# A hand-written order for two transformer layers: turns of TensorE in one piece, and other constants in the planner

## What is computed

```
for l in (0, 1):
    sa, ca, ga, sb, cb, gb = split(silu(c[l]) @ wmod[l])       # per batch, 256 each
    ga, gb = sign(ga) * max(|ga|, 0.25), sign(gb) * max(|gb|, 0.25)
    h = layernorm(x) * (1 + ca) + sa
    x = x + ga * attention[l](h)                               # 16 heads of 16, causal
    h = layernorm(x) * (1 + cb) + sb
    x = x + gb * ffn[l](h)
```

## Time and profile before

| | |
|---|---|
| median of 3 runs | 2705.45 us (2704.71 to 2705.87) |
| the profiled execution | 2702.86 us |
| its span, first to last instruction | 2701.1 us |
| mean granted clock of PE | 0.968 of full |
| PE busy | 2432.1 us (90%), 18968 matmuls |
| DVE busy | 2127.8 us (79%) |
| ACT busy | 1701.9 us (63%) |
| POOL busy | 1025.6 us (38%) |
| DMA | 218.38 MB, mean 81 GB/s |

### The profile page before, as it was taken

The page is one execution under the profiler, slowest core; times in us unless marked ns, Lnnn a source line. Parts: engine busy times, 40 slices in busy tenths (PEclk is TensorE's granted clock), DMA queues, the critical chain, the costliest instruction groups (busy, mean ns, idle before and its releaser), DMA issues. The chain is left out here.

```text
span 2701.1 us, 56435 instructions
## 1 busy us (share of the span) xinstructions
PE 2432.1 (90%) x18968; PEld 1023.9 (38%) x18968; DVE 2127.8 (79%) x6588; ACT 1701.9 (63%) x3458; POOL 1025.6 (38%) x1558
## 2 busy tenths in 40 slices
PE   7798888999999999999999999999999999898586
PEld 4323434324334343443434343343434434344223
DVE  3898738898887988879887888879888798862972
ACT  3476574576765667666676677666677666665164
POOL 4222452245332544236243453325342363326222
PEclk9999999999999999999999999999999999999798
DMA  6511134113322222322312133222223123002300
GB/s 219 166 58 35 38 109 119 47 44 103 105 81 75 79 88 89 92 72 83 116 61 83 51 102 105 83 81 72 91 88 102 60 83 109 21 31 74 97 2 16
DMA packets 142400, 218.38 MB, mean 81 GB/s; under 512 B 21190, under 2 KB 62556, under 8 KB 142052
## 3 DMA queue, kind: packets, MB, share of 16 engines
q1 hardware_dynamic: 142120, 214.77, 25.9%
HBM read 137.87 MB, written 77.89 MB: 80 GB/s over the span
## 5 line engine op out<-in xcount | busy, mean ns | idle before, releaser
L1208 ACT ACTIVATE probs<-big 128x512 f32<-128x512 f32 (+2 forms) x2560 | 1218.9, 573 | 457.1 <-PE big L1656 451.5
L1421 DVE CUSTOM_DVE_ANT_0 big<-big,mask 128x128 f32<-128x128 f32 (+3 forms) x2048 | 940.0, 518 | 157.3 <-PE big L1634 155.0
L1656 PE MATMUL big<-stack_q,stack_k 64*128 64x512 f16 (+3 forms) x6144 | 684.6, 330 | 69.6 <-DVE mx L1421 27.0
L1419 DVE TENSOR_REDUCE mx<-big 128x1 f32<-128x512 f32 x1024 | 644.0, 679 | 119.2 <-PE big L1634 115.1
L1675 PE MATMUL ctx_ps<-probs,v_ones 128*17 128x512 f32 (+3 forms) x6144 | 645.3, 501 | 28.2 <-POOL probs L1087 26.6
L1087 POOL TENSOR_SCALAR_AFFINE_SELECT probs<-probs 128x512 f32<-128x512 f32 x512 | 332.5, 660 | 591.1 <-ACT probs L1208 590.9
L1634 PE MATMUL big<-stack_k,stack_q 64*128 64x512 f16 (+3 forms) x3072 | 434.9, 332 | 74.7 <-DVE mx L1421 39.5
L1656 PEld LDWEIGHTS big<-stack_q,stack_k 64*128 64x128 f16 x6144 | 222.5, 94 | 668.9 <-issue 470.9
L1634 PEld LDWEIGHTS big<-stack_k,stack_q 64*128 64x128 f16 x3072 | 136.3, 94 | 410.8 <-issue 254.3
L1421 DVE DVE_READ_ACCUMULATOR2_ANT mx<- 128x1 f32 x2048 | 282.8, 138 | 0.0
L1580 PE MATMUL big<-hT,w_qkv 128*128 128x512 f32 x512 | 266.4, 629 | 1.4 <-DVE mx L1421 0.5
(11 more groups left out here) (94 smaller groups left out, 1923.3 us busy)
## 6 DMA issues: line engine op xcount, KB each, us to landing
image<-region SPq DMA_DIRECT2D x192, 256.0 KB
stack_q<-image SPq DMA_DIRECT2D x64, 512.0 KB, 3.7
stack_k<-image SPq DMA_DIRECT2D x64, 512.0 KB, 4.5
lo_dram<-region SPq DMA_DIRECT2D x64, 256.0 KB
w_qkv<-wqkv SPq DMA_DIRECT2D x16, 768.0 KB, 4.9
x_res<-x SPq DMA_DIRECT2D x32, 256.0 KB, 2.9
stack_q<-lo_dram SPq DMA_DIRECT2D x128, 64.0 KB, 3.8
stack_k<-lo_dram SPq DMA_DIRECT2D x128, 64.0 KB, 4.5
```

Of the source, the lines that this page charges most:

```text
L1208: s.activation(probs[:, n % HELD, heads, q0:], big[:, at.slot(turn), 0:len(pairs) * width] .rearrange("p (h q) -> p h q", h=len(pairs)), A ...
L1419: last = v.reduce_max(to, held, AX)
L1421: last = v.tensor_tensor_reduce(out=held, in0=held, in1=mask[:, BANK - width:], scale=1.0, scalar=3.0 * NEG, op0=ALU.add, op1=ALU.max, acc ...
L1656: last = te.matmul(big[:, at.slot(at.turn() + parity), j * width:(j + 1) * width], stack_k[rows, c, g * PAIR_N + pair, kt * P:(kt + 1) * P ...
```

## The change

The planner no longer puts halves into its queues: the `pre` and `post` queues hold each turn once, and `pe_time` gives it its whole cost. In the model, a link of the layernorm chain on POOL costs 200 ns of the engine and 85 ns on top until the next may begin, where it was 77 and 110 on both engines; on DVE it stays so. The constants `ROWS_FIRST`, `PHASES` and `FEED_WAIT` have other values. The instructions themselves are the same; only their order changes. (The added line moves all lines behind it by one: L1580 before is L1581 after.)

```diff
@@ pe_time
-    return pe_cost(item) / (2 if kind in HALVED else 1)
+    return pe_cost(item)
@@
-ROWS_FIRST = 445.6080
+ROWS_FIRST = 520.8978
@@
-PHASES = {"max": (-0.0897, 0.0000, 0.0000, 0.0000, 0.0000, 0.0000, 0.0000, 0.0514), ...
-FIRST_FEED, FEED_WAIT = {"max": 216.0, "score": 430.0}, 300.0000
+PHASES = {"max": (-0.0897, 0.0000, 0.0000, 0.1674, 0.0207, 0.0000, 0.0000, 0.0514), ...
+FIRST_FEED, FEED_WAIT = {"max": 216.0, "score": 430.0}, 264.0094
@@ Model.other, "ln"
-                self.ready["ln"] = self.ready["factors"] = self.run(engine, begin, 75 * (item[6] - item[5]) if n == 0 else 77, 110)
+                self.ready["ln"] = self.ready["factors"] = self.run(engine, begin, 75 * (item[6] - item[5]) if n == 0 else 77 if engine == "DVE" else 200,
+                                                                              110 if engine == "DVE" else 85)
@@ plan
-        queues[name] = [x for u in units for i in parts(u) for x in ([("half", i[1], i), i] if i[0] in HALVED else [i])]
+        queues[name] = [x for u in units for i in parts(u) for x in [i]]
```

More of the change, by code:

```diff
@@ L212 @@
 FEED = {"DVE": 0.0215, "ACT": 0.1346}
-ROWS_FIRST = 445.6080
+ROWS_FIRST = 520.8978
 def ease(engine):
     return CHAIN_EASE if engine == "DVE" else EASE
-PHASES = {"max": (-0.0897, 0.0000, 0.0000, 0.0000, 0.0000, 0.0000, 0.0000, 0.0514), "pre": (0.0000, 0.0000, 0.0000, 0.1303, 0.0000, 0.0000, 0.0000, 0.0000), "post": (0.0000, 0.0000, -0.3023, 0.0000, -0.0043, 0.0000, 0.1945, 0.0000)}
-FIRST_FEED, FEED_WAIT = {"max": 216.0, "score": 430.0}, 300.0000
+PHASES = {"max": (-0.0897, 0.0000, 0.0000, 0.1674, 0.0207, 0.0000, 0.0000, 0.0514), "pre": (0.0000, 0.0000, 0.0110, 0.1303, 0.0000, 0.0000, 0.0000, 0.0000), "post": (0.0000, 0.0000, -0.3023, 0.0000, -0.0043, 0.0232, 0.1945, 0.0000)}
+FIRST_FEED, FEED_WAIT = {"max": 216.0, "score": 430.0}, 264.0094
 NORM_ON = ("DVE", "DVE", "POOL", "DVE")
```

## The result

The changed kernel takes 2697.53 us (median of 7 runs, 2691.98 to 2699.42), the kernel before 2705.87 us beside it (2704.71 to 2707.52). The ratio is 0.9962, with a 95% interval of 0.9952 to 0.9971: faster by 0.3 to 0.5%, some 8 to 10 us. I had forecast 27 us less, 2678. The direction was right and the time lies in the range, but the gain is about a third of what was forecast.

What follows compares the result with a forecast made beforehand. The prediction took TensorE (PE) to bound the kernel. Fewer shape changes (-25 us), the layernorm chain's cost (-6) and coarser pieces (+4) summed to -27, from 2705.45 to 2678 us; range 2654 to 2707.

Steps and rivals of the forecast that it cites:

- (a): TensorE's array shape: fewer changes between 64-row, 128-row and 32-column work cut its busy time, -25 us.
- (b): Layernorm chain on POOL costed at its length: mask waits go, partly offset by later `xn`, -6 us.
- (c): TensorE's 122 formerly split turns, now whole: coarser pieces feed DVE later, mostly covered by banked work, +4 us.
- the row at 742.39: DVE's 1.19 us idle after one whole `qk` turn in the old trace, where TensorE had no wait.
- The second rival: After each of 122 joined turns: whole turns starve the feeders, 0.37 us each, making it slower, 2720 us; chance 0.12.
- The first rival: At banks DVE has not emptied: TensorE arrives earlier and DVE takes back half to all, 2693 to 2705; chance 0.22.
- (d): Planner constants ROWS_FIRST, PHASES, FEED_WAIT: only move which item comes next, so no price of their own.

Runs made afterwards that it cites:

- join_early: The kernel before, in its old order, with each split turn's two halves joined at the first half's place: 2731.11 us, ratio 1.0097.
- join_late: The kernel before, in its old order, with each split turn's two halves joined at the second half's place: 2749.93 us, ratio 1.0164.
- join_single: The kernel before with only the 54 split turns joined that had a single max item between their halves: 2722.41 us, ratio 1.0062.
- join_early_lite: The kernel before with split turns joined at the first half and maxima outside the mask over a quarter of the columns: 2678.99 us, ratio 0.9899.
- after_split: The changed kernel with 89 qk and value turns cut in two again, the following max item between the halves: 2709.91 us, 1.0013 of the kernel before.
- after_halved: The changed kernel with halves put back into the queues, new constants and chain cost kept: 2746.30 us, 1.0146 of the kernel before.
- chain_only: The kernel before with only the new POOL cost of the layernorm chain, halves and old constants kept: 2783.47 us, ratio 1.0291.
- whole_only: The kernel before with only whole turns in the planner's queues, old constants and chain cost kept: 2763.00 us, ratio 1.0208.
- after_oldconst: The changed kernel with the old ROWS_FIRST, PHASES and FEED_WAIT: 2715.06 us, 1.0033 of the kernel before.
- before_lite: The kernel before with maxima outside the mask taken over a quarter of the columns, order untouched: 2654.94 us, ratio 0.9810.

## Why the prediction was wrong, step by step

**(a) Fewer shape changes: right in kind, -25 forecast, -19.8 measured.** This is within the 15 to 30 that I gave, at the same clock of 0.968. The 0.31 us a round trip is a little high. In join_early the busy time fell by 29.3 us for 89 round trips (27.6 by the price), but in join_late by 10.4 for as many, in join_single by 4.4 for 50 (15.5 by the price), in join_early_lite by 9.2 for 89, and in after_split it rose by 18.4 for 78 (24 by the price). The clocks differ among these. With each busy time multiplied by its mean clock, an estimate, the five come to 0.23 to 0.33 us a round trip.

**(b) The chain costed at its length: right in kind, and mis-sized.** I took -6 us. At the place that I showed, 1.29 us became 0.20 and 2.20 became 0.29. Over the run PE's waits for `xn` fell by 17.0 us and for the mask by 9.4, 26.4 us in all, where I had feared that `xn` would come later and cost. But this isn't a gain of 26 us: the same edit alone made the kernel 78 us slower. In an order that is planned as a whole, the wait that goes in one place isn't the edit's worth.

**(c) PE's waits for its feeders: this is the step that failed.** I took +4 us for coarser pieces, because "the row at 742.39 is the nearest and shows cover", and wrote that PE's waits for the maxima and for `probs` would grow by no more than 10 us. Those for the maxima rose by 35.4, from 92.8 to 128.2; those for `probs` on ACT fell by 7.2, so the sum rose by 28.2. Two mistakes are in the step.

The first is the sample. I priced a joined turn from turns that stood whole in the old order. There the planner's prices had put nothing between the halves; at the 122 places that it had split they had put something there. Joined in place, those 122 turns cost 0.45 us of idle PE each, 54.8 us in all, of which the waits for `mx` have 44.5. The five whole turns that I had read showed 0.13.

The second is that I gave the whole rise to the joined turns and let all else stand. The runs don't bear this out. after_halved has halves and still waits 125.5 us for `mx`, chain_only has halves and waits 149.9, and whole_only, with nothing but whole turns, waits 102.1. Cutting 89 turns of the changed kernel in two again took only 9.3 us off. The four kernels that have the new cost of the chain and none of my own constants wait 121 to 150 us for `mx`, before and whole_only 93 and 102. So the rise comes with the new order as a whole and goes with the new cost of the chain more than with whole turns; which of the planner's choices make it isn't shown.

The second rival had a mechanism that is real in a fixed order ("whole turns starve the feeders"; it decides from 0.25 us a turn, and 0.45 was measured), but the changed kernel isn't a fixed order, and it didn't get slower. The first rival had the sum: busy time down and waits for DVE up by as much or more, and 2697.53 us lies in its range of 2693 to 2705. I gave them 0.12 and 0.22.

**(d) The constants: "priced by (a) to (c)" was wrong too.** With whole turns and the new chain, the old constants give 2715.06 us and the new 2697.53: 17.5 us, more than twice the whole gain. I had treated them as a rearrangement without a price. Most of the 17.5 goes with busy time and with the granted clock, which I had left out of the sum; between before and the changed kernel the clock is in fact the same.

**The sum.** The busy time fell by 19.8 us. The waits for `xn` and the mask fell by 26.4 and those for the maxima rose by 35.4; the rest cancels, and the idle time rose by 8.9. This gives the -10.9 us of span. Against my sum, (a) gave 5 us less and (b) 20 more than I took, and the waits for the maxima, for which I had +4, took 31 more. That the time still fell in my range owes something to luck: two errors of 20 and 31 us stood against each other.

Shown is that joining turns in the old order costs more than it saves because of the maxima behind them: the price goes from +25 us to -14 as these are shortened. Shown is also that the change as a whole owes its sign to the constants (after_oldconst). Argued, and not shown, is that the changed kernel's gain is held back by the same contention for DVE: relief of DVE raises it from 8 to 25 us, some 18 with the clock allowed for, but little of this is waits. Left open are which of the constants does it, and what in an order sets the granted clock.

## What to carry to other kernels

A piece of work that the old schedule had cut may have been cut at a place that needed it; its price when whole is not that of the pieces that were whole already, so measure it at the cut ones, in the fixed order. Count what a longer piece does to the engine that it feeds: at the place shown, saving 0.2 us on TensorE was worth nothing where VectorE then stood idle for 0.9 us more, with masked maxima queued behind it. Edits to a greedy planner don't add up: whole turns lost 57 us with one cost of the layernorm chain and gained 68 with the other. Ask the planner for its own finishing time before a run is spent. And where its constants were found by search, compare forms only after each has had its own search: at fixed constants the edits moved the time by up to 78 us, with constants of their own the two forms differ by 7.

## What the runs showed of the hardware

At the places looked at, going from 64-row matmuls to 128-row float32 ones and back costs 0.31 us, 0.20 us with the 128-row turn and 0.11 with the 64-row work; over whole kernels it comes to 0.23 to 0.33 us, an estimate with the clocks allowed for. TensorE's busy time is not a measure of its work alone: with the same 18968 matmuls it ran from 2402.8 us (join_early, granted clock 0.971) to 2467.0 us (chain_only, 0.954), so two orders can't be compared by it without the clock beside it. The clock isn't all either: before and before_lite have the same order and clocks of 0.968 and 0.969, and their busy times are 2432.1 and 2410.2 us. An order has a granted clock of its own: the six runs of after_oldconst lie at 0.955 to 0.958, the seven of the changed kernel at 0.965 to 0.970.
